# Segment scan on one Trainium2 core: the local product moves to eight array tiles and one step later, and the output projection is done per four batches

## The reference

```python
def step(carry, inp):                     # 16 segments of 32 positions, in order
    mem, z = carry
    q_s, k_s, v_s, qn_s, kn_s = inp       # q_s, k_s with rotary positions, qn_s, kn_s without
    scores = jnp.where(mask, einsum('bhnd,bhmd->bhnm', q_s, k_s) * SCALE, -inf)
    sdpa = einsum('bhnm,bhmd->bhnd', softmax(scores), v_s)      # the local product
    sq = elu1(qn_s)
    mem_out = einsum('bhnk,bhkv->bhnv', sq, mem) / (einsum('bhnk,bhk->bhn', sq, z)[..., None] + 1e-6)
    out = beta * mem_out + (1.0 - beta) * sdpa
    sk = elu1(kn_s)
    prev_v = einsum('bhnk,bhkv->bhnv', sk, mem) / einsum('bhnk,bhk->bhn', sk, z)[..., None]
    mem = mem + einsum('bhnk,bhnv->bhkv', sk, v_s - prev_v)
    z = z + sk.sum(axis=2)
    return (mem, z), out
x = x + outs @ w_out + (fake_quant_fp8(xn) @ fake_quant_fp8(weight).T + bias)
```

## Time and profile before

| what | value |
|---|---|
| time, median of 3 runs | 3117.67 us (3115.82 to 3118.49) |
| the profiled execution, own time | 3123.61 us |
| its span on the core | 3121.8 us |
| busy in the span: PE, DVE, ACT, POOL | 2667.9, 2507.4, 1875.7, 1760.6 us |
| granted TensorE clock over the span | 0.936 |
| 2400 to 2700 us: PE, DVE, ACT, POOL busy, clock | 276.22, 255.35, 153.07, 248.04 us; 0.99 |

### The profile page before, as it was taken

One profiled execution on the slowest core, in us unless ns is written; L12 is line 12 of the kernel. 1 busy time (PEld: TensorE's weight loads), 2 busy tenths in 40 slices (PEclk: granted clock), 3 DMA queues, 4 the chain that ended last, 5 costly groups with the idle time before them and its releaser, 6 DMA issues. The chain is left out here.

```text
span 3121.8 us, 129631 instructions
## 1 busy us (share of the span) xinstructions
PE 2667.9 (85%) x53553; PEld 1513.3 (48%) x53553; DVE 2507.4 (80%) x7598; ACT 1875.7 (60%) x3797; POOL 1760.6 (56%) x1988
## 2 busy tenths in 40 slices
PE   5787999999999999872331899999999999999998
PEld 2342333333333333372230666666666666666665
DVE  4678898999999999586606888888888888888886
ACT  5785999999999999630001555555445555455543
POOL 5773222222222222240063888888888888888886
PEclk9896999999999999995655999999999999999999
DMA  4656444444444443192023000000000000000000
GB/s 127 211 199 174 94 94 94 96 101 93 90 93 95 106 94 87 33 325 60 6 41 93 4 11 11 11 11 5 11 11 11 11 11 11 11 11 4 11 8 11
DMA packets 173633, 201.58 MB, mean 65 GB/s; under 512 B 31152, under 2 KB 134512, under 8 KB 172784
## 3 DMA queue, kind: packets, MB, share of 16 engines
q1 hardware_dynamic: 170480, 191.87, 23.8%
q0 software_dynamic: 2560, 1.35, 0.4%
HBM read 125.10 MB, written 67.24 MB: 62 GB/s over the span
## 5 line engine op out<-in xcount | busy, mean ns | idle before, releaser
L845 ACT ACTIVATE at_pA<-at_ps 128x512 f32<-128x512 f32 x1024 | 552.2, 615 | 57.7 <-DVE at_ps L897 51.0
L906 DVE CUSTOM_DVE_ANT_0 at_junk<-at_ps,w_cmask 128x512 f32<-128x512 f32 (+3 forms) x1024 | 463.2, 485 | 102.5 <-PE at_ps L748 95.0
L897 DVE TENSOR_TENSOR at_ps<-at_ps,w_ratio 128x128 f32<-128x128 f32 (+3 forms) x1024 | 451.0, 491 | 2.1 <-PE at_ps L742 0.5
L714 POOL TENSOR_SCALAR_AFFINE_SELECT at_pB<-at_pB 128x128 f32<-128x128 f32 x256 | 74.8, 292 | 639.8 <-ACT at_pB L851 637.8
L851 ACT ACTIVATE at_pB<-at_ps 128x512 f32<-128x512 f32 (+1 forms) x768 | 379.8, 532 | 52.8 <-PE at_ps L755 47.5
L1995 POOL TENSOR_TENSOR sc_rb<-sc_rb,v_sin 128x512 f32<-128x512 f32 x256 | 326.0, 1273 | 43.1 <-DVE sc_ra L2235 42.0
L2031 PE MATMUL sc_ps<-sc_xT,v_wqkv 128*128 128x512 f32 x512 | 288.5, 646 | 4.6 <-issue 2.0
L742 PE MATMUL at_ps<-at_aq,at_ak 72*128 72x512 bf16 x1024 | 278.6, 388 | 0.4 <-DVE at_mx L906 0.2
L2194 ACT COPY sc_skN<-sc_ps 128x512 f32<-128x512 f32 x128 | 75.0, 586 | 324.7 <-PE sc_ps L2083 324.7
L1990 POOL TENSOR_TENSOR sc_sk<-sc_ee,sc_relu 128x512 f32<-128x512 f32 x128 | 165.6, 1294 | 184.9 <-ACT sc_ee L2185 184.8
L755 PE MATMUL at_ps<-at_bq,at_bk 75*128 75x512 bf16 (+3 forms) x1024 | 265.7, 302 | 1.5 <-ACT at_pB L851 0.9
(11 more groups left out here) (317 smaller groups left out, 5955.9 us busy)
## 6 DMA issues: line engine op xcount, KB each, us to landing
parts_scratch<-fr_parts SPq DMA_DIRECT2D x64, 384.0 KB, 4.1
at_bk<-parts_scratch SPq DMA_DIRECT2D x192, 96.0 KB
at_ak<-parts_scratch SPq DMA_DIRECT2D x192, 96.0 KB
v_scratch<-fr_v SPq DMA_DIRECT2D x32, 352.0 KB, 4.4
at_v<-v_scratch SPq DMA_DIRECT2D x32, 352.0 KB, 3.5
at_bq<-parts_scratch SPq DMA_DIRECT2D x128, 64.0 KB
at_aq<-parts_scratch SPq DMA_DIRECT2D x128, 64.0 KB
on_scratch<-at_on SPq DMA_DIRECT2D x32, 256.0 KB, 2.2
```

The source lines that it names most:

```text
L845: act.activation(pA[:, n % A_RING, j * S:(j + 1) * S], src, ACT.Exp).then_inc(exped, 1)
L897: dve.tensor_tensor(src[:, 0:wide], src[:, 0:wide], W["ratio"][:, S - wide:S], ALU.mult).then_inc(tilted, 1)
L906: ins = dve.tensor_tensor_reduce(junk[:, P * j * (j + 1) // 2:P * (j + 1) * (j + 2) // 2], src[:, col:col + wide], W["cmask"][:, S - wide: ...
```

## The change

It has six parts, all of them in `scan`.

1. **Local product.** The four tiles become eight and the bank becomes two: for odd groups g the result of batch f goes to columns (and partitions) of batch f^1 (`swapped`), and to bank 7 in place of 6. So the odd groups' outputs lie in another order of batches; RQ, the loads and stores, `hb` and the quantized operand follow that order.
2. **One step later.** L works on unit s-3 in place of s-2, and stands behind V and ahead of RK. The wait for `pt` stays.
3. **Probabilities divided before.** VectorE sums the exponentials and takes the reciprocal (`smd`), GpSimd multiplies the probabilities by it (new, 128x256, `nrm`), and VectorE transposes them at the head of the next step (`pt`).
4. **Who handles the result.** The scaling by (1 - beta) goes from VectorE to ScalarE (two ACTIVATEs, 128x256 each, from both banks, `old`); the sum with the memory part goes from GpSimd to VectorE (`od`). On VectorE the second `rope` of a step now comes behind the sum and reciprocal.
5. **Output projection.** `oT` keeps a whole segment. In place of one product of 512 columns per step, each step does four products of 128 columns, which gather four of the eight pairs for one group of four batches, straight in the output's order. VectorE adds each result (128x128) to `y`, so in every step. `turn_y`, the copy `yT` and the sum of 512 columns go. The last segment's eight half sums run after its last pair, so `STEPS` grows from 133 to 138.
6. **DMAs.** `hb` is loaded on its own, by 8 DMAs per segment; stores are 8 per segment, not 4; the loads stand ahead of the store wait in SP's queue. `take_xq` becomes three copies.

```diff
-        STEPS = PT + 5
+        HALVES, AFTER = 2 * BG, PAIRS + 2
+        STEPS = PT + AFTER
+        out_half = lambda s: (divmod((s - AFTER) % HALVES, 2), (s - AFTER) // HALVES) if inside(s - AFTER) else None
...
+        def load_hb(sp, seg, j):
+            for f in range(B1):
+                for odd in range(2):
+                    to = 32 * swapped(odd, f)
+                    sp.dma_start(hb[to:to + 32, j % 2, odd::2], h_seg[f, bass.ds(seg, 1)].rearrange("o i g d -> (o i) g d")[:, odd::2]).then_inc(G[f"hb_in{j % 2}"], 16)
...
@@ GpSimd
-                        p = s - 2
+                        p = s - 3
                         if inside(p):
                             new = uu[:, p % PAIRS, :, :, 0:DH]
...
+                        p = s - 1
+                        if inside(p):
+                            wait(pool, "smd", p + 1)
+                            probs = ss[:, p % 2].rearrange("p (g h) j -> p g h j", h=2)
+                            pool.tensor_tensor(probs, probs, bc(by_ch(sm[:, p % 4]), SEG), ALU.mult).then_inc(G["nrm"], 1)
...
-                            pool.tensor_tensor(o, o, t2[:, p % 2].rearrange("p c d -> p (c d)"), ALU.add).then_inc(G["od"], 1)
@@ TensorE
                     def local(p):
-                        for g in range(BG):
-                            for hh in range(2):
+                        for hh in range(2):
+                            for g in range(BG):
                                 for f in range(B1):
-                                    ins = pe.matmul(ps[32 * f:32 * f + 32, 6, ch * DH:(ch + 1) * DH], pT[32 * f:32 * f + 32, p % 4, ch, :],
+                                    ch, to, col = 2 * g + hh, 32 * swapped(g, f), (2 * (g // 2) + hh) * DH
+                                    ins = pe.matmul(ps[to:to + 32, 6 + g % 2, col:col + DH], pT[32 * f:32 * f + 32, p % 4, ch, :],
...
+                    def project_out(j, g, half):
+                        few = range(half * PAIRS // 2, (half + 1) * PAIRS // 2)
+                        for h in few:
+                            ins = pe.matmul(ps[:, 7, YCOL:YCOL + D], oT[:, j % 2, h, g * P:(g + 1) * P], V["wout"][:, h], start=(h == few[0]), stop=(h == few[-1]))
+                        ins.then_inc(G["oproj"], 1)
...
-                        p = s - 2
+                        if s < PT:
+                            values(s)
+                        p = s - 3
                         if inside(p):
                             wait(pe, "otc", min(s - 3, PT))
+                            wait(pe, "ydone", s - AFTER)
                             wait(pe, "pt", p + 1)
                             local(p)
-                        if s < PT:
-                            values(s)
...
-                            wait(pe, "old", min(s - 1, PT))
+                            wait(pe, "old", min(s - 2, PT))
                             wait(pe, "sgk", p + 1)
                             turn_keys(p)
@@ ScalarE
+                            for hh in range(2):
+                                col = 2 * (p % PAIRS) + hh
+                                ins = act.activation(to[:, :, :, hh], local[:, :, :, hh], ACT.Identity, scale=V["rest"][:, col:col + 1])
+                            ins.then_inc(G["old"], 1)
@@ VectorE
-                                ins = dve.scalar_tensor_tensor(ol[:, p % 4, :, hh], local[:, :, hh], V["rest"][:, col:col + 1],
-                                                               bc(head(sm[:, p % 4])[:, hh], DH), ALU.mult, ALU.mult)
+                            wait(dve, "nrm", p + 1)
+                            dve.transpose(pT[:, p % 4].rearrange("p c j -> p (c j)"), ss[:, p % 2].rearrange("p c j -> p (c j)")).then_inc(G["pt"], 1)
...
+                            dve.tensor_tensor(o, o, t2[:, p % 2].rearrange("p c d -> p (c d)"), ALU.add).then_inc(G["od"], 1)
...
+                            dve.tensor_tensor(y[:, j % 2, g], y[:, j % 2, g], ps[:, 7, YCOL:YCOL + D], ALU.add).then_inc(G["ydone"], 1)
```

More of the change, by code:

```diff
@@ L1892, in take_xq @@
             wait(act, "xqt", n)
-            act.copy(xqT[:, j % 2], ps[:, bank, 0:256].bitcast(BF16)).then_inc(G["xqt_c"], 1)
+            place = lambda ap: ap.rearrange("p (q o a b i) -> p q o a b i", q=2, o=2, a=2, b=2)
+            to, at = place(xqT[:, j % 2]), place(ps[:, bank, 0:256].bitcast(BF16))
+            act.copy(to[:, :, 0].rearrange("p q a b i -> p q (a b i)"), at[:, :, 0].rearrange("p q a b i -> p q (a b i)"))
+            for b in range(2):
+                ins = act.copy(to[:, :, 1, :, 1 - b], at[:, :, 1, :, b])
+            ins.then_inc(G["xqt_c"], 1)
         def prepare(seg):
@@ L1901, in _ @@
                     load(sp, seg, 0)
+                    load_hb(sp, seg, 0)
                 @block.vector
@@ L2015, in _ @@
                         for j in at_step(s, 3):
-                            wait(pool, "ffn_c", j - 1)
                             add_bias(pool, j)
-                        p = s - 2
-                        if inside(p):
-                            wait(pool, "qd", p + 1)
-                            wait(pool, "old", p + 1)
-                            o = ol[:, p % 4].rearrange("p g h d -> p (g h d)")
-                            pool.tensor_tensor(o, o, t2[:, p % 2].rearrange("p c d -> p (c d)"), ALU.add).then_inc(G["od"], 1)
                 @block.tensor
@@ L2089, in turn_heads @@
                         ins.then_inc(G["ott"], 1)
-                    def project_out(p):
-                        wait(pe, "otc", p + 1)
-                        wait(pe, "yt_c", p // PAIRS)
-                        h = p % PAIRS
-                        pe.matmul(ps[:, 7, :], V["wout"][:, h], oT[:, p % 2], start=(h == 0), stop=(h == PAIRS - 1)).then_inc(G["oproj"], 1)
-                    def turn_y(bank, j):
-                        wait(pe, "yt_c", j + 1)
-                        for g in range(BG):
-                            ins = pe.transpose(ps[:, bank, g * P:(g + 1) * P], yT[:, g * P:(g + 1) * P], V["ident"][:])
-                        ins.then_inc(G["yt"], 1)
+                    def project_out(j, g, half):
[3 more added lines that the diff above has]
+                        ins.then_inc(G["oproj"], 1)
                     for s in range(STEPS):
@@ L2136, in _ @@
                             recall(p, 0, "qr_s")
-                        p = s - 4
-                        if inside(p):
-                            project_out(p)
+                        if out_half(s):
+                            (g, half), j = out_half(s)
+                            wait(pe, "old", min(s - 2, PT))
+                            wait(pe, "otc", j * PAIRS + 4 * half + 4)
+                            wait(pe, "ydone", s - AFTER)
+                            project_out(j, g, half)
                         p = s - 3
@@ L2204, in _ @@
                             features(2 * s + 1)
-                        p = s - 4
-                        if inside(p) and p % PAIRS == PAIRS - 1:
-                            wait(act, "oproj", p + 1)
-                            wait(act, "yt", p // PAIRS)
-                            act.copy(yT[:], ps[:, 7, :]).then_inc(G["yt_c"], 1)
                         p = s - 3
@@ L2212, in _ @@
                             wait(act, "ott", p + 1)
-                            wait(act, "oproj", p - 1)
-                            act.copy(oT[:, p % 2], ps[:, 6, :]).then_inc(G["otc"], 1)
+                            if p // PAIRS >= 2 and p % PAIRS == 0:
+                                wait(act, "oproj", HALVES * (p // PAIRS - 1))
+                            act.copy(oT[:, p // PAIRS % 2, p % PAIRS], ps[:, 6, :]).then_inc(G["otc"], 1)
                         for j in at_step(s, 3):
@@ L2286, in _ @@
                             round_fp8(dve, link, j)
+                        p = s - 3
+                        if inside(p):
+                            wait(dve, "old", p + 1)
+                            wait(dve, "qd", p + 1)
+                            o = ol[:, p % 4].rearrange("p g h d -> p (g h d)")
+                            dve.tensor_tensor(o, o, t2[:, p % 2].rearrange("p c d -> p (c d)"), ALU.add).then_inc(G["od"], 1)
                         p = s - 2
```

67 lines of the change are left out of this document (33 added, 34 removed).

## The result

| | before | after |
|---|---|---|
| time, median | 3117.12 us (3115.82 to 3118.49, 4 runs) | 3169.64 us (3153.44 to 3172.82, 4 runs) |
| profiled execution, own time; span | 3123.61; 3121.8 us | 3172.82; 3170.1 us |
| first P1 to the end of the last step / 127 | 10.84 us | 11.09 us |
| last P1 to the end of the span | 34.3 us | 46.5 us |

The account below looks back on a forecast made before the run. TensorE was taken to be bound by its products plus holes while instruction blocks arrive, 3.6 us each. Usual steps +30, rounding steps +10, relief -10 and end +8 made +38 us: 3156 us, range 3090 to 3198.

Parts of the forecast that it names:

- denser blocks: TensorE's instruction stream, L and RK now neighbours: blocks run through before the next is fetched, +0.41 us per step.
- L on eight tiles: L's products on TensorE, eight tiles for four: 0.82 us for 1.03, -0.21 per step (bounds -0.24 and 0).
- L behind V: P1 on TensorE, now followed by V on the whole array: -0.10 us per step.
- TK waits for ACT: TK on TensorE waits for ScalarE's scaling of L's result, hidden only by RK: +0.21 us per step.
- Work of PE: TensorE's work in a usual step, without TK's wait: -0.35 us.
- rope behind the sum: VectorE's second rope ends later while V needs its bank earlier: 0, at most 0.1 us per step.
- od and the lock: VectorE's od sum and its lock with GpSimd: hidden in usual steps, +10 us over the rounding steps.
- rival C: VectorE's od meets GpSimd in each step and waits its 1.26 us in full: 3196 us, chance 0.11.
- The relief: Other waits shrink because VectorE no longer waits for L: -10 us.
- PO: Output projection on TensorE, eight records of 128 columns: +0.02 us per step; turn_y gone: -0.06.
- the end's +8: Behind the last pair: six more steps, more stores, less some work gone, about +8 us.
- Rival B: Holes do not depend on order, so TensorE's saving reaches the step: 3108 to 3081 us, likeliest 3096, chance 0.27.

Follow-up runs that it names:

- run 11: Kernel before, with PO cut to 64 of 512 columns for six of the eight pairs, same number of instructions: 3117.41 us, ratio to before 1.0036.
- run 9: Changed kernel with L's products in four tiles again, everything else of the change kept: 3160.00 us, ratio to before 1.0173.
- run 1: Changed kernel with V put back between L and RK on TensorE: 3145.73 us, ratio to before 1.0111.
- run 2: Changed kernel with TK moved behind S on TensorE: 3173.62 us, ratio to before 1.0197.
- run 12: Kernel of run 1 with VectorE's second rope ahead of sum and reciprocal, division behind GpSimd's second rotate, transposition behind sigma_q: 3135.62 us, ratio to before 1.0100.
- Run 6: Kernel before with only the new output projection of the change, including its sums for y and longer end: 3140.47 us, ratio to before 1.0096.
- Run 10: Kernel of Run 6 with the second half of the heads summed in the bank, VectorE adding every second step: 3132.03 us, ratio to before 1.0089.
- run 5: Kernel before with V moved ahead of L on TensorE and nothing else changed: 3154.39 us, ratio to before 1.0141.
- run 3: Changed kernel with the od sum moved from VectorE to GpSimd, behind the first rotate of the step: 3176.15 us, ratio to before 1.0207.

## Why the prediction was right, and where its numbers were off

The forecast was slower, 3156, from denser blocks; the time is 3169.64, inside the range. The sum of 38 is 52.5 measured. The direction was right and the mechanism is at work, but that the sums come this near is in part luck: the denser blocks, 46 us in a sum of 38, came out at half their size, while the output projection, 3 us in the sum, cost 24 to 35, and the clock was no term at all.

Two of the prediction's supports are weaker than they look. A step of 344 records is 2.71 blocks whatever bounds it, so the mean interval of the packets is the step over 2.71, and "2.71 x 3.99 = 10.8" gives back the step that was put in. And the 0.46 per step to which the 3.6 us was fitted are the two largest groups; all "issue" holes of the scan were 74.2 us, 0.58 per step. What does speak for a fetch time is the shortest distance between two packets of this queue: 3.29 us in the scan of before, of after and of run 11 alike.

- **L on eight tiles**, -0.21: the rate came out at -0.24. Its worth in time is nil (run 9).
- **L behind V**, -0.10: P1 to RK is 0.27 shorter with V first (run 1), its wait for the rope included.
- **TK waits for ACT**, +0.21: RK to TK is 1.00 for 0.79, exactly that; the scalings take 0.47 each, not 0.43, and overlap. That this wait is a price by itself is not borne out: without it M waits for POOL instead (run 2).
- **Work of PE** without waits, -0.35: it was -0.22 (0.25 of the step less 0.47 of idle time), with 0.05 for the lower clock in it, so some -0.27 at the same clock.
- **The clock**: not in the sum. Behind the 12th step 13.6 us more at the lower level, 5 us by the estimate, or 0.05 per step.
- **Denser blocks**, +0.41: mis-sized. "Issue" grew by 25.9 us, 0.20 per step. The mechanism is shown from both sides: thinning the stretch with V takes 23 us of holes from S (run 1), with a slower L 23 us from PE as a whole, with no change in time (run 9). One reason for the size is that the model let nothing but blocks hold PE up, while 0.27 per step of other waits came with the change; that a wait takes the place of a hole is what run 11 shows. How much of the missing 0.21 it explains is not measured. And the holes do not lie in L's and RK's records, as the text had it, but in S: a block that starts in L ends there. The Trainium skill, "Runtime: NRT & Kernel Launch", section Instruction fetch mechanics, calls the crossing of such a boundary "mostly hidden"; with 74 to 100 us of PE's idle time in the scan put down to "issue", nearly all of its holes on the beat of 127 records, the traces of this case disagree.
- **rope behind the sum**, 0 to 0.1: 13.2 + 5.8 us of PE's idle time, 0.15 per step, a little over the bound; but taking P1's part away gains nothing that can be measured (run 12).
- **od and the lock**: `od` at 0.79 (0.7 to 1.0 expected), rival C out. The rounding step grew from 12.21 to 12.85 us, x 16 = 10.2, the +10 of the sum. **The relief** of 10 us didn't show: DVE no longer waits for L, but for S, 118.5 us for 26.2 before.
- **PO**, +0.02 - 0.06 per step: this is the term most off. Run 6 puts the new projection at 24 to 35 us, with the end's +8 in it (8.9 there, 12.2 in after). Run 10 leaves at most 10 us for VectorE's sums, likeliest 2, and the clock has no part (13.7 us at the lower level for 17.1). What remains, some 15 to 20 us, is open: a candidate is the six more records per step, 6 / 127 of a block of 3.99, 0.19 us per step, if the mean rate of blocks counts. No kernel here changed the number of records alone, and the profiled execution of run 6 has only 0.08 per step.
- **Rival B** (the saving reaches the step) failed: run 9 shows it for L, and run 11 for the 66 us of work in the kernel before, of which 38 came back as idle time and some 9 through the clock.

If the ratios simply add, the loss of 1.62% is made of 0.96% for the projection (run 6), 0.51% for V's place (run 1), and 0.15% for all the rest, L's new tiles and lag, the division, ScalarE and `od`; the last is no more than the intervals. That they add isn't shown: the same move of V costs 1.41% in the kernel before (run 5). What stays open beside PO is which of the two, the rate of blocks or VectorE's chain behind RQ, would set the step if the other were gone: both were still there in run 11.

## What to carry to other kernels

When an engine is nine tenths busy, ask of each part what it covers before making it faster: here PO covers VectorE's reading, TK GpSimd's rotation, and V covers ScalarE's pass and thins out the instruction stream. A part made faster between two others of many small products gives a hole at the next border. A kernel with the work at that place cut out (run 11) tells in one run how much of a saving there comes back as waits. Read the granted clock beside it: in these traces it fell behind waits of TensorE, and a part of what is saved can go that way.

## What was unexpected

The blocks of 127 product records show in after as in before. Its instruction queue, 1720 to 3125 us (packets, MB, share):

```profile
q8 instruction: 348, 5.70, 1.7%
```

That is one packet per 4.04 us, for 3.99 before and 3.96 with 66 us of work gone. These means only follow the step, as said above. A saving on the busiest engine can come with a lower clock of that engine: run 11 has the least work on PE and, with runs 2 and 3, the most time at 1.2 GHz. Sixty-four products of 32 by 32 by 64 took 0.79 us over eight tiles of two banks and 1.03 over four tiles of one, in the same surroundings.
